# A cross-attention and expert kernel on one core: eight constant matmuls for ten, VectorE for all low parts of the query weights, and a new order on every engine

## The chip, the core and the metric

The kernel runs on one core of a Trainium2 chip. The metric is the device time of one execution in microseconds (us), taken over repeated runs; the core has five engines that matter here: TensorE (PE in the profile, with its weight loads as PEld), VectorE (DVE), ScalarE (ACT), GpSimd (POOL) and SyncE (SP), which only issues the DMAs. The engines run their own instruction streams in order and meet through semaphores.

## What is computed

A block of cross-attention with a residual, and then a small mixture of experts with a residual, for x of 4 x 512 x 512 and a context of 4 x 64 x 512, in float32. Cut to what matters:

```python
h  = layernorm(x)                                  # over 512 features
q  = h @ Wq.T + bq ; k = ctx @ Wk.T + bk ; v = ctx @ Wv.T + bv     # 16 heads of 32
s  = clip(q k / sqrt(32), -50, 50), -10000 where masked, clip again
c  = softmax(s) v
d  = rs * (c @ Wo.T + bo)
x1 = x + (d - mean(d)) / sqrt(var(d) + eps) * gamma + beta
n  = layernorm(x1)
g  = softmax(n @ router.T), kept for the 2 largest of 8 experts
x2 = x1 + sum over experts of g_e * silu(n @ down_e.T) @ up_e
```

## The kernel before

The rows of x are taken in four batches of four tiles of 128 rows; `f(b, t)` below is step f for batch b and tile (or chunk, or half) t. All data stay in SBUF. A float32 product that has to be exact enough is made of three passes of the rounded type fp32r: operands are split into a high part (ACT casts, `hs_hi`, `wq_high`, `att_hi`) and a low part (a subtraction, `hs_lo`, `wq_low`, `wo_low`, `att_lo`), and `passes` issues hi x hi, hi x lo and lo x hi for each of four chunks: 12 matmuls of 128 x 512 for `query` and for `project`.

The order of the start on PE: WARM constant matmuls of 128 x 128 on the tile `average` (float32, so two passes each), `keys(c)` and `values(c)` for the four chunks of context weights, the transposes of the normalised tiles of batch 0 (`hs_transpose`, at L496), then `query(0, 0..3)`, then the transposes of batch 1, `scores(0, 0)`, `expert_means` and `scores(0, 1)`, and `query(1, 0)`. `query(b, 0)` waits for all four low parts of the batch (`hst_lo`, written at L1119 by VectorE for batches 0 and 1), and for all four `wq_lo` chunks.

On VectorE the start is: the cleaning of the context (`clean_marks`, `clean_limited`, `clean_finite`), the layernorm statistics (`tile_stats`, L1262 and L1264), `hs_lo(0, t)`, the mask (`mask_limits`), two of the four `wq_low` (L1284), the statistics of batch 1, the centring of the output weights in place (`centre_wo(c)`, whose last step is L1274), the blocks of values (`value_blocks`, L1163), `hs_lo(1, t)` and the clipping of the exponentiated scores (`clip`, L1178). GpSimd forms the other two `wq_low` (L1584), adds beta to the residual in place (`add_beta`, L1530) after its DMA, raises variances to the power -1/2 (`ln_power`), and forms `up_lo`, `wo_lo` and `attt_lo` (L1589, L1579, L1534).

Each engine's order is written out by hand, call by call. The eight PSUM banks are handed from use to use by the table `BANKS`: a row is a bank, a name a use (K keys, Q query, S scores, W projection, U and E experts' up products, h, n, a transposes, V values, m means, s sums, v weighed values, f down products), and a use may begin when the engine that reads out the use before it is done (`take`, and `seed` for W and E). Where the names are on one row, one waits for the other:

```python
        def take(use):
            before = banks.before(use)
            if before:
                pe.wait_ge(freeing[before[0]], banks.count(before))
            return bank(use)
```

Lines that the steps below touch: L635 constant matmuls, L529 keys, L539 values, L496 transposes, L478 all matmuls that `passes` issues, L555 scores, L569 sums, L1119, L1163, L1178, L1262, L1274, L1284 on VectorE, L1530, L1584 on GpSimd.

## Time and profile before

| | |
|---|---|
| median of 3 runs | 182.28 us (182.18 to 182.46) |
| the profiled execution, its own time | 181.53 us |
| its span in the profile | 179.7 us |
| busy: PE, DVE, ACT, POOL | 171.3, 133.0, 118.5, 106.7 us |
| share of the chain that ended last: PE, DVE | 51%, 26% |
| granted TensorE clock | 1.00 over nearly all of the span |

The span goes from the first to the last record of the profiled execution; 1.83 us of that execution's time lie outside it. Times in the rows are counted from the start of the span. A row of the timeline has start, length, engine, line, operation, what is written <- what is read, and in brackets how long the engine sat idle before and what it waited for. Two neighbouring instructions of one engine may overlap by some 0.07 us, so four of a kind take a little less than four times one.

### The profile page before, as it was taken

The numbers are of one execution on the slowest core, as the hardware profiler recorded it, in microseconds if no ns is written. First come the engines' busy times: TensorE is split into PE (matmuls) and PEld (weight loads), VectorE is DVE, ScalarE is ACT, GpSimd is POOL, SyncE is SP. The second block draws the span as 40 slices with busy tenths as digits, with TensorE's granted clock in tenths as the row PEclk, the third lists the DMA queues.
The fourth block names the chain that finished last, engine by engine and source line by source line (L and its number), as shares of the span: only waits on it lengthen the run. The fifth ranks groups of instructions, "written<-read, shape, count | busy, mean of one in ns | idle before, by whom it ended". The sixth has DMA issues, their size and how long they took to land.

```text
span 179.7 us, 3565 instructions
## 1 busy us (share of the span) xinstructions
PE 171.3 (95%) x1212; PEld 126.2 (70%) x1212; DVE 133.0 (74%) x300; ACT 118.5 (66%) x239; POOL 106.7 (59%) x159
## 2 busy tenths in 40 slices
PE   7999899978999999999999999999999999999992
PEld 7766578646845477688788687657876688889861
DVE  3695999997999389769148784075999985877891
ACT  3038818865736768469998575379935767688852
POOL 6042899974765617999987983066143692385200
PEclk9999999999999999999999999999999999999999
DMA  4999993000249974355990248621143598001068
GB/s 161 329 395 368 383 357 121 0 0 4 53 151 305 314 160 135 117 181 205 311 227 14 119 133 252 175 60 62 26 109 127 181 330 254 2 2 58 2 226 303
DMA packets 18050, 30.14 MB, mean 168 GB/s; under 512 B 3056, under 2 KB 8176, under 8 KB 17776
## 3 DMA queue, kind: packets, MB, share of 16 engines
q1 hardware_dynamic: 18032, 29.92, 51.5%
q8 instruction: 10, 0.16, 0.4%
q14 instruction: 8, 0.07, 0.1%
HBM read 19.95 MB, written 9.96 MB: 166 GB/s over the span
## 4 chain that ended last, share of the span: by engine, by line
PE 51%; DVE 26%; DMA 8%; SPq 7%; issue 3%; ACT 2%; POOL 1%; DVEq 0%; ACTq 0%
PE ps L478 43%; DMA mask_sb<-mask_t 4%; DVE ln_st L1262 2%; PE ps L555 2%; PE ps L569 2%; DVE stage L1178 2%; DVE hst_lo L1119 2%; DMA x_scratch<-x_turned 2%; DVE rz L1183 2%; DVE v_sb L1163 2%; DVE wq_lo L1284 2%; PE ps L583 2%; PE ps L496 2%; DMA x_turned<-x_scratch 2%; DVE xs L1274 1%
## 5 line engine op out<-in xcount | busy, mean ns | idle before, releaser
L478 PE MATMUL ps<-hst_hi,wq_hi 128*128 128x512 f32 x64 | 25.9, 405 | 1.7 <-DVE hst_lo L1119 1.7
L1534 POOL TENSOR_TENSOR attt_lo<-wk,attt_hi 128x512 fp32r<-128x512 f32 x16 | 21.1, 1346 | 9.6 <-ACT attt_hi L813 9.6
L478 PE MATMUL ps<-wo_hi,attt_hi 128*128 128x512 f32 x64 | 26.0, 406 | 0.3 <-POOL attt_lo L1534 0.3
L478 PE MATMUL ps<-wo_hi,attt_lo 128*128 128x512 f32 x64 | 25.3, 395 | 0.0
L478 PE MATMUL ps<-hst_lo,wq_hi 128*128 128x512 f32 x64 | 25.3, 395 | 0.0
L478 PE MATMUL ps<-hst_hi,wq_lo 128*128 128x512 f32 x64 | 25.3, 395 | 0.0
L478 PE MATMUL ps<-wo_lo,attt_hi 128*128 128x512 f32 x64 | 25.3, 395 | 0.0
L1530 POOL TENSOR_TENSOR xs<-xs,beta_bc 128x512 f32<-128x512 f32 x16 | 20.7, 1324 | 1.7 <-ACT hs L776 0.9
L1178 DVE TENSOR_SCALAR stage<-stage,exp_max 128x1024 f32<-128x1024 f32 x16 | 13.9, 881 | 8.8 <-ACT stage L795 8.8
L776 ACT ACTIVATE hs<-xs,ln_bias,ln_rstd 128x512 f32<-128x512 f32 x16 | 12.1, 808 | 11.8 <-POOL ln_bias L1522 11.8
L795 ACT ACTIVATE stage<-ps 128x1024 f32<-128x1024 f32 x16 | 16.1, 1021 | 4.4 <-PE ps L555 4.4
L478 PEld LDWEIGHTS ps<-hst_hi,wq_hi 128*128 128x128 f32 x64 | 12.0, 188 | 8.3 <-issue 3.6
L782 ACT ACTIVATE q_sb<-ps,bq_sb 128x512 f32<-128x512 f32 x16 | 10.7, 682 | 9.9 <-PE ps L478 9.8
L478 PEld LDWEIGHTS ps<-dr_raw,x1t 128*128 128x128 f32 x128 | 15.5, 190 | 1.7 <-issue 1.1
L1549 POOL TENSOR_SCALAR d_ve<-d_sq,rs_sq 128x1 f32<-128x1 f32 x16 | 4.6, 289 | 20.3 <-ACT cen L876 19.9
L478 PE MATMUL ps<-dr_raw,x1t 128*128 128x136 f32 x128 | 16.3, 282 | 0.1
L1188 DVE TENSOR_TENSOR wk<-ps,wk 128x512 f32<-128x512 f32 x16 | 10.4, 677 | 7.3 <-PE ps L583 6.3
L478 PEld LDWEIGHTS ps<-wo_hi,attt_hi 128*128 128x128 f32 x64 | 12.0, 188 | 4.2 <-issue 1.7
L1205 DVE SCALAR_TENSOR_TENSOR xs<-cen,d_rstd,xs 128x512 f32<-128x512 f32 x16 | 11.9, 748 | 3.7 <-POOL d_rstd L1552 3.7
L813 ACT CAST attt_hi<-wk 128x512 fp32r<-128x512 f32 x16 | 9.7, 620 | 7.0 <-DVE wk L1188 4.8
L876 ACT ACTIVATE cen<-ps 128x512 f32<-128x512 f32 x16 | 9.5, 594 | 6.9 <-PE ps L478 6.6
L478 PEld LDWEIGHTS ps<-hst_hi,wq_lo 128*128 128x128 f32 x64 | 12.0, 188 | 2.8
(114 smaller groups left out, 395.6 us busy)
## 6 DMA issues: line engine op xcount, KB each, us to landing
wk<-rz_scratch SPq DMA_DIRECT2D x32, 128.0 KB, 2.8
out<-xs SPq DMA_DIRECT2D x16, 256.0 KB, 2.6
xs<-x SPq DMA_DIRECT2D x3, 1024.0 KB, 8.4
x_scratch<-x_turned SPq DMA_DIRECT2D x6, 512.0 KB, 2.6
x_turned<-x_scratch SPq DMA_DIRECT2D x24, 128.0 KB, 2.8
hs_scratch<-hs_turned SPq DMA_DIRECT2D x2, 1024.0 KB, 4.6
hs<-hs_scratch SPq DMA_DIRECT2D x8, 256.0 KB, 5.6
wk<-wk_t SPq DMA_DIRECT2D x4, 256.0 KB, 6.5
```

The lines of the kernel that those rows point to most:

```text
L478: last = pe.matmul(dst, w, m, start=start and i == 0, stop=stop and i == n - 1, skip_group_check=unseen)
L776: act.activation(hs[:, t, :], xs[:, bass.ds(tile, 1), :], ACT.Identity, bias=ln_bias[:, bass.ds(tile, 1)], scale=ln_rstd[:, bass.ds(tile, ...
L782: act.activation(q_sb[:, m, :], bank(f"Q{b}{m}"), ACT.Identity, bias=bq_sb[:, m:m + 1]).then_inc(q_ok, 1)
L795: act.activation(probs[:, 2 * c:2 * c + 2, :], bank(f"S{b}{2 * c}", 2).rearrange("p (c n) -> p c n", c=2), ACT.Exp, scale=SCALE).then_inc( ...
L813: act.copy(attt_hi[:, :, c, :], att[:, c, :].rearrange("p (t n) -> p t n", t=NT)).then_inc(attt_hi_ok, 1)
L876: act.activation(cen[:, t, :], bank(f"W{b}{t}"), ACT.Square, accum_out=d_sq[:, NT * b + t:NT * b + t + 1]).then_inc(d_sq_ok, 1)
L1178: dve.tensor_scalar(probs[:, ps, :], probs[:, ps, :], EXP_LO, exp_max[:, b:b + 1], ALU.max, ALU.min).then_inc(probs_ok, 1)
L1188: dve.tensor_tensor(att[:, c, :], bank(f"v{b}{c}"), att[:, c, :], ALU.mult).then_inc(weighed_out, 1)
L1205: dve.scalar_tensor_tensor(x_tile, cen[:, t, :], d_rstd[:, NT * b + t:NT * b + t + 1], x_tile, ALU.mult, ALU.add, accum_out=n_sum[:, NT * ...
L1530: pool.tensor_tensor(xt, xt, beta_bc[:, :], ALU.add).then_inc(xb_ok, 1)
L1534: pool.tensor_tensor(attt_lo[:, :, c, :], att[:, c, :].rearrange("p (t n) -> p t n", t=NT), attt_hi[:, :, c, :].bitcast(F32), ALU.subtract ...
L1549: pool.tensor_scalar(d_ve[:, NT * b + t:NT * b + t + 1], d_sq[:, NT * b + t:NT * b + t + 1], rs_sq[:, :], EPS, ALU.mult, ALU.add).then_inc ...
```

## The change

1. WARM is 8, was 10.
2. The last two `wq_low` chunks move from GpSimd to VectorE, which now forms all four; `wq_low(0)` stands ahead of `mask_limits`, the other three behind it.
3. New orders. On PE `keys(2)` moves ahead of `hs_transpose(0, 0)`, `scores(0, 1)` ahead of `expert_means`, and some steps of the later batches change places by one to three positions; on ACT, VectorE and GpSimd likewise. SP swaps one fetch with one send of reciprocals.
4. New rows in `BANKS`. The uses of late batches sit on other banks; `U12 U13 U20 U22` now follow each other on one bank.

The arithmetic is that of before: same operations, same shapes, apart from the two constant matmuls whose result nobody reads.

```diff
-WARM = 10
+WARM = 8
...
-    "K3 S00 S05 Q12 S13 S16 W03 S20 W11 S26 Q33 S33 S36 W23 U10 W32 U13 U22",
+    "K2 Q03 S04 Q11 S12 S15 W02 Q23 W10 S25 Q32 S32 S36 W23 U10 W32 U12 U13 U20 U22",
...
             keys(1)
+            keys(2)
             hs_transpose(0, 0)
-            keys(2)
...
+            scores(0, 1)
             expert_means()
-            scores(0, 1)
...
             hs_norm(0, 1)
+            hs_norm(0, 2)
             hs_hi(0, 0)
-            hs_norm(0, 2)
...
             clean_marks(3)
-            hs_lo(0, 0)
             clean_limited(3)
             clean_finite(3)
+            hs_lo(0, 0)
             hs_lo(0, 1)
+            wq_low(0)
             mask_limits()
-            wq_low(0)
             wq_low(1)
+            wq_low(2)
+            wq_low(3)
...
             ln_power(2, 4)
-            wq_low(2)
-            wq_low(3)
             add_beta(0, 0)
```

VectorE between the context cleaning and the statistics of batch 1; `hst_lo` are the low parts of the normalised tiles of batch 0, `dr_raw` and `compare` hold the context's marks and its clean copy, `attend` and `exp_max` are the mask. The first fence is before, the second the changed kernel.

```order
L1119 TENSOR_TENSOR hst_lo<-ps,hst_hi 128x512
L1301 COPY_PREDICATED compare<-dr_raw,hidden 128x256
L1305 COPY_PREDICATED compare<-dr_raw,stage 128x256
L1119 TENSOR_TENSOR hst_lo<-ps,hst_hi 128x512
L1309 TENSOR_SCALAR attend<-mask_sb 128x4
L1311 TENSOR_SCALAR exp_max<-attend 128x4
L1284 TENSOR_TENSOR wq_lo<-stage,wq_hi 128x512 x2
L1119 TENSOR_TENSOR hst_lo<-ps,hst_hi 128x512 x2
```

```order
L1301 COPY_PREDICATED compare<-dr_raw,hidden 128x256
L1305 COPY_PREDICATED compare<-dr_raw,stage 128x256
L1119 TENSOR_TENSOR hst_lo<-ps,hst_hi 128x512 x2
L1284 TENSOR_TENSOR wq_lo<-stage,wq_hi 128x512
L1309 TENSOR_SCALAR attend<-mask_sb 128x4
L1311 TENSOR_SCALAR exp_max<-attend 128x4
L1284 TENSOR_TENSOR wq_lo<-stage,wq_hi 128x512 x3
L1119 TENSOR_TENSOR hst_lo<-ps,hst_hi 128x512 x2
```

VectorE has two more subtractions here, and `hst_lo` of tile 0 stands behind the cleaning of the last context chunk instead of inside it.

VectorE from the statistics of batch 2 to the clipping of batch 0's scores (`stage`); the `hst_lo` are now those of batch 1.

```order
 L1262 BN_STATS ln_st<-xs 128x6
 L1264 BN_AGGR ln_mv<-ln_st 128x2
-L1119 TENSOR_TENSOR hst_lo<-ps,hst_hi 128x512
-L1178 TENSOR_SCALAR stage<-stage,exp_max 128x1024
-L1119 TENSOR_TENSOR hst_lo<-ps,hst_hi 128x512 x2
-L1178 TENSOR_SCALAR stage<-stage,exp_max 128x1024
-L1262 BN_STATS ln_st<-xs 128x6
-L1264 BN_AGGR ln_mv<-ln_st 128x2
-L1178 TENSOR_SCALAR stage<-stage,exp_max 128x1024 x2
+L1178 TENSOR_SCALAR stage<-stage,exp_max 128x1024
+L1119 TENSOR_TENSOR hst_lo<-ps,hst_hi 128x512 x3
+L1262 BN_STATS ln_st<-xs 128x6
+L1264 BN_AGGR ln_mv<-ln_st 128x2
+L1178 TENSOR_SCALAR stage<-stage,exp_max 128x1024 x3
```

The first clip moves ahead of `hs_lo(1, 1)`, and the second behind the statistics of the last tile of batch 2.

## Rows read from the trace of the kernel before

**Rows 1.** Page: busy time by engine, and the chain's shares by engine.
```profile
PE 171.3 (95%) x1212; PEld 126.2 (70%) x1212; DVE 133.0 (74%) x300; ACT 118.5 (66%) x239; POOL 106.7 (59%) x159
PE 51%; DVE 26%; DMA 8%; SPq 7%; issue 3%; ACT 2%; POOL 1%; DVEq 0%; ACTq 0%
```
**Rows 2.** Stretches: start:end, length, busy us (instructions) by engine, granted clock, DMA.
```profile
30.00:40.00 10.00, 8.91 (x74) 6.18 (x72) 9.58 (x19) 8.48 (x14) 9.29 (x8) 1.00 0.01 2
62.00:172.00 110.00, 109.83 (x785) 83.94 (x785) 78.99 (x192) 80.83 (x181) 66.34 (x100) 1.00 0.45 137
```
**Rows 3.** PE's longest wait in all, over the whole span: us, times, longest.
```profile
PE ps L478 <- DVE hst_lo L1119: 2.4, 3, 1.0
```
**Rows 4.** Timeline of PE, the first 13 us.
```profile
1.05 4.63 PE L635 MATMUL ps<-average 128*128 128x128 f32 x20 [1.05 <-POOL average L1592]
5.47 1.93 PE L529 MATMUL ps<-compare,wk 128*128 128x256 f32 x8
11.00 1.99 PE L529 MATMUL ps<-compare,wk 128*128 128x256 f32 x8 [0.17 <-DMA wk<-wk_t]
```
**Rows 5.** Timeline of DVE, POOL, ACT and PE around the query weights.
```profile
17.63 0.17 DVE L1309 TENSOR_SCALAR attend<-mask_sb 128x4 f32<-128x4 int32 x1 [0.68 <-DMA mask_sb<-mask_t]
17.91 3.46 DVE L1284 TENSOR_TENSOR wq_lo<-stage,wq_hi 128x512 fp32r<-128x512 f32 x2
17.86 2.96 POOL L1584 TENSOR_TENSOR wq_lo<-stage,wq_hi 128x512 fp32r<-128x512 f32 x2 [3.17 <-ACT wq_hi L894]
19.51 1.07 ACT L759 CAST hst_hi<-ps 128x512 fp32r<-128x512 f32 x2 [0.51 <-PE ps L496]
21.29 1.27 DVE L1119 TENSOR_TENSOR hst_lo<-ps,hst_hi 128x512 fp32r<-128x512 f32 x2
19.74 1.89 PE L529 MATMUL ps<-compare,wk 128*128 128x256 f32 x8
22.66 0.47 PE L478 MATMUL ps<-hst_hi,wq_hi 128*128 128x512 f32 x1 [1.03 <-DVE hst_lo L1119]
```
**Rows 6.** Groups of one line: ns min/median/max, first and last start.
```profile
L1294 DVE TENSOR_TENSOR dr_raw<-stage x4: 414/418/420, 3.4 to 13.2; 128x256 uint8<-128x256 f32 x4
```
**Rows 7.** Timeline of DVE and POOL, 21 to 32 us.
```profile
21.62 5.02 POOL L1530 TENSOR_TENSOR xs<-xs,beta_bc 128x512 f32<-128x512 f32 x4 [0.80 <-DMA beta_bc<-beta]
26.66 0.49 DVE L1274 TENSOR_SCALAR xs<-xs,w_mv 128x512 f32<-128x512 f32 x1
29.12 1.29 POOL L1589 TENSOR_TENSOR up_lo<-hidden,up_hi 128x512 fp32r<-128x512 f32 x1
29.49 1.22 DVE L1274 TENSOR_SCALAR xs<-xs,w_mv 128x512 f32<-128x512 f32 x1
```
**Rows 8.** Timeline of POOL, DVE and PE, 36 to 42 us.
```profile
36.79 2.50 POOL L1579 TENSOR_TENSOR wo_lo<-xs,wo_hi 128x512 fp32r<-128x512 f32 x2
36.14 0.69 DVE L1119 TENSOR_TENSOR hst_lo<-ps,hst_hi 128x512 fp32r<-128x512 f32 x1
38.14 1.71 DVE L1178 TENSOR_SCALAR stage<-stage,exp_max 128x1024 f32<-128x1024 f32 x1
39.77 1.27 DVE L1119 TENSOR_TENSOR hst_lo<-ps,hst_hi 128x512 fp32r<-128x512 f32 x2
38.28 1.19 PE L478 MATMUL ps<-dr_raw,average 128*128 128x136 f32 x8 [0.67 <-DVE hst_lo L1119]
41.19 0.47 PE L478 MATMUL ps<-hst_hi,wq_hi 128*128 128x512 f32 x1 [0.67 <-DVE hst_lo L1119]
```
**Rows 9.** Timeline of POOL, DVE and PE, 46 to 62 us.
```profile
46.19 5.07 POOL L1530 TENSOR_TENSOR xs<-xs,beta_bc 128x512 f32<-128x512 f32 x4 [0.93 <-ACT hs L776]
49.92 1.63 DVE L1274 TENSOR_SCALAR xs<-xs,w_mv 128x512 f32<-128x512 f32 x1
61.77 0.47 PE L478 MATMUL ps<-wo_hi,attt_hi 128*128 128x512 f32 x1 [0.26 <-POOL attt_lo L1534]
```
**Rows 10.** Timeline of PE at the end.
```profile
172.90 0.44 PE L496 MATMUL ps<-ident,hidden 128*128 128x128 f32 x2 [0.31 <-DVE hidden L1245]
```

More of the change, by code:

```diff
@@ L707, in _ @@
             project(2, 1)
+            weigh(3, 0)
             sums(3, 1)
             project(2, 2)
-            weigh(3, 0)
+            project(2, 3)
             hid_transpose(0, 1)
-            project(2, 3)
+            weigh(3, 1)
             up(0, 1)
             hid_transpose(1, 0)
-            weigh(3, 1)
             up(0, 2)
@@ L735, in _ @@
             x1_transpose(3, 2)
+            up(1, 2)
             down(3, 0)
             down(3, 1)
+            up(1, 3)
+            x1_transpose(3, 3)
+            hid_transpose(2, 1)
             down(3, 2)
-            x1_transpose(3, 3)
-            up(1, 3)
-            hid_transpose(2, 1)
             down(3, 3)
@@ L931, in _ @@
             exp_scores(0, 0)
+            exp_scores(0, 1)
             hs_hi(1, 1)
[L933 removed]
             hs_hi(1, 2)
@@ L986, in _ @@
             exp_scores(2, 0)
+            exp_scores(2, 1)
             seed(1, 1)
             seed(1, 2)
-            exp_scores(2, 1)
             seed(1, 3)
             x1_out(0, 2)
+            down_scaled(0, 0)
             projected_squares(1, 0)
-            down_scaled(0, 0)
+            x1_out(0, 3)
             down_scaled(0, 1)
-            x1_out(0, 3)
+            hidden_tanh(0, 0)
             exp_logits(0, 0)
-            hidden_tanh(0, 0)
             projected_squares(1, 1)
@@ L1012, in _ @@
             x1_out(1, 0)
+            x1_out(1, 1)
+            hid_hi(0, 0)
+            query_out(3, 1)
             x1_squares(1, 3)
-            query_out(3, 1)
-            x1_out(1, 1)
             query_out(3, 2)
             query_out(3, 3)
+            exp_scores(3, 0)
             att_hi(2, 0)
             att_hi(2, 1)
-            exp_scores(3, 0)
+            exp_scores(3, 1)
+            down_scaled(0, 2)
             att_hi(2, 2)
             att_hi(2, 3)
-            down_scaled(0, 2)
+            down_scaled(0, 3)
             x1_out(1, 2)
-            exp_scores(3, 1)
             x1_out(1, 3)
+            hidden_tanh(0, 1)
             seed(2, 0)
-            down_scaled(0, 3)
-            hidden_tanh(0, 1)
             exp_scores(3, 2)
@@ L1067, in _ @@
             projected_squares(3, 0)
+            x1_squares(2, 3)
             x1_out(2, 2)
@@ L1070, in _ @@
             x1_out(2, 3)
+            experts_seed(2, 3)
             projected_squares(3, 1)
-            x1_squares(2, 3)
-            experts_seed(2, 3)
+            x1_squares(3, 0)
+            projected_squares(3, 2)
+            x1_squares(3, 1)
+            experts_seed(3, 1)
+            x1_squares(3, 2)
             hid_hi(1, 1)
-            projected_squares(3, 2)
-            x1_squares(3, 0)
-            x1_squares(3, 1)
             hid_hi(2, 0)
+            down_scaled(2, 2)
             projected_squares(3, 3)
-            down_scaled(2, 2)
-            x1_squares(3, 2)
             down_scaled(2, 3)
@@ L1085, in _ @@
             x1_out(3, 1)
+            x1_out(3, 2)
             exp_logits(2, 1)
-            x1_out(3, 2)
+            experts_seed(3, 2)
+            down_scaled(3, 0)
             x1_squares(3, 3)
-            down_scaled(3, 0)
             down_scaled(3, 1)
@@ L1365, in _ @@
             tile_stats(2, 2)
+            clip(0, 0)
             hs_lo(1, 1)
-            clip(0, 0)
             hs_lo(1, 2)
             hs_lo(1, 3)
+            tile_stats(2, 3)
             clip(0, 1)
-            tile_stats(2, 3)
             clip(0, 2)
@@ L1404, in _ @@
             product(1, 0)
+            product(1, 1)
             residual(0, 1)
@@ L1423, in _ @@
             residual(1, 0)
-            gating(0, 0)
+            x1_turn(1, 0)
             scaled(1, 1)
-            x1_turn(1, 0)
-            scaled(1, 2)
             residual(1, 1)
             x1_turn(1, 1)
+            scaled(1, 2)
+            gating(0, 0)
             scaled(1, 3)
-            reciprocals(2, 0)
             residual(1, 2)
             clip(2, 2)
+            reciprocals(2, 0)
+            clip(2, 3)
             x1_turn(1, 2)
-            clip(2, 3)
+            residual(1, 3)
             hid_lo(0, 0)
-            residual(1, 3)
             x1_turn(1, 3)
@@ L1441, in _ @@
             product(2, 1)
+            clip(3, 0)
             product(2, 2)
             product(2, 3)
-            clip(3, 0)
+            clip(3, 1)
             finish(0, 0)
-            clip(3, 1)
             largest(0, 1)
@@ L1465, in _ @@
             residual(2, 2)
+            hid_lo(0, 1)
             x1_turn(2, 2)
             scaled(2, 3)
+            product(3, 2)
             hid_lo(1, 0)
-            product(3, 2)
             finish(0, 1)
+            product(3, 3)
             finish(0, 2)
-            product(3, 3)
             residual(2, 3)
@@ L1627, in _ @@
             add_beta(1, 2)
+            wo_low(1)
             add_beta(1, 3)
-            wo_low(1)
             wo_low(2)
```

51 lines of the change are left out of this document (22 added, 29 removed), and 14 rows, old and new, of the table BANKS.

## The prediction, written before the changed kernel was run

> **What bounds the kernel now.** I read the page's busy times and chain first, then the busy time by stretch, then TensorE's waits, then the timelines of the places where it waits. TensorE is busy for 171.3 of 179.7 us and carries 51% of the chain that ended last; VectorE carries another 26% [rows 1]. The stretches say where each of the two rules. From 62 to 172 us TensorE is busy for 109.83 of 110 us, so in there an order can only lose time, never gain it [rows 2]. What can be gained is ahead of that: from 30 to 40 us TensorE is busy for 8.91 us and VectorE for 9.58 [rows 2], and nearly all that TensorE waits for is `hst_lo`, VectorE's low parts of the normalised rows: 2.4 us in three waits [rows 3], at 22.66, 38.28 and 41.19 us [rows 5, 8]. One more short wait for `attt_lo` ends at 61.77 [rows 9], and one for the gating at 172.90 [rows 10]. So the sum is made at two points: when `query(0, 0)` starts (22.66) and when `query(1, 0)` starts (41.19), and after that at the start of the projections (61.77).
>
> **Two constant matmuls fewer.** Twenty passes take 4.63 us, 0.23 each [rows 4], so four fewer take 0.9 us off TensorE's first work. The keys' first matmuls can move forward by that at most, but the second chunk of key weights lands only at 11.00, where TensorE already waits 0.17 us for it [rows 4]; the gain ends there. Worth nothing on the path: the cover is that DMA, and if the DMA came earlier the gain would be up to 0.9. The passes still run until about 4.8, and the keys follow with hardly a hole, so TensorE is as busy as before when it reaches its steady pace.
>
> **All low parts of the query weights on VectorE.** Before, VectorE takes 3.46 us for two chunks, 1.73 each, while GpSimd takes 2.96 us for its two over the same time [rows 5]. With GpSimd out of there, what does one cost? The nearest row is the comparison of a context chunk with itself, also two float32 inputs from SBUF, of 256 elements: 418 ns [rows 6]; the subtraction of 512 elements from PSUM takes 0.69 alone and 1.27 for a pair, 0.61 in a series [rows 8, 5]. Lower end 0.61, upper end 1.73 (that of before, if the length were the instruction's own); I take 0.61 to 0.7, since the 418 ns are twice 0.21, and 512 elements at that rate are under 0.84.
> The row says that the two engines' subtractions hold each other up. The Trainium skill (SBUF — State Buffer, section "Who interferes with whom") states the rule: a VectorE instruction with two SBUF inputs contends with a GpSimd instruction that reads SBUF, and one waits until the other is through. By that rule a chunk is short once GpSimd is silent; without it the upper end would stand.
> Then the step: one chunk fits into the 0.68 us that VectorE idled ahead of the mask, three stand behind the mask, which ends at 18.0 [rows 5]. 18.0 + 3 x 0.61 to 0.7 = 19.8 to 20.1. The last two high parts are done at 20.58 [rows 5], the first of them at about 20.1, and each `hs_lo` takes 0.61: 21.35 to 21.5. Placing `keys(2)` ahead of the transposes delays ScalarE's casts of the weights by some 0.3 us and not its last two. TensorE itself is through with the last keys at 19.74 + 1.89 = 21.63 [rows 5]. So TensorE becomes what ends last, and `query(0, 0)` starts at 21.6 to 21.8: 0.9 to 1.0 us earlier. VectorE is ahead of its old place by 22.56 - 21.4 = 1.1 us.
>
> **GpSimd is not earlier for it.** It loses 2.96 us of work, but its next step, `add_beta(0, 0)`, waited 0.80 us for beta, which lands at 21.6 [rows 7]. So its four additions of 1.25 us still run from 21.62 to 26.64 with no hole.
>
> **What VectorE's lead meets.** `centre_wo(0)` ends in a scalar subtraction that took 0.49 us at 26.66, just after these additions, and 1.22 at 29.49, when `up_lo` ran on GpSimd until 30.41 [rows 7]: this operation, too, waits for GpSimd. 1.1 us earlier it comes at 25.5, and the fourth addition runs from 25.37 to 26.64. So it waits until 26.64 and VectorE's lead is gone: it reaches the values' blocks at 30.6 as before. TensorE, ahead by 1.0, then waits that much longer for the slot that `hs_lo(1, 0)` frees at 36.8 [rows 8]. The order of the statistics and values changes nothing in that sum.
>
> **Clip ahead of `hs_lo(1, 1)`.** Before, the first clip comes at 38.2, meets `wo_low` and takes 1.71 us, to 39.85, of which only the 0.56 after GpSimd's end at 39.29 can be work; the last two `hs_lo` follow from 39.77 to 41.04 and `query(1, 0)` at 41.19 [rows 8]. Now the clip comes at 37.55. GpSimd is full of additions and subtractions of 1.25 us until 39.29, and the next border between two of them is at 38.05 [rows 8]. In the pair of query weights the engines took turns at such borders, so I let the clip in there: 38.05 to 38.65, then three `hs_lo` of 0.61, 40.5. `expert_means` (1.19 us) needs the first of these, at 39.3, and is through at 40.5 as well; `scores(0, 1)` now fills its wait of 0.67 [rows 8]. `query(1, 0)` starts at 40.55: 0.64 earlier. Bounds: 1.76 + 1.03 = 2.8 us earlier if VectorE never held TensorE (1.76 is the 1.09 us of TensorE's idle time from 30 to 40 us [rows 2] and the 0.67 at 41.19; 1.03 the wait at 22.66 [rows 5]), 0.55 later if the clip gets in only at 39.29.
>
> **To the projections.** VectorE's next steps start with TensorE's sums and move with it. `centre_wo(3)` at 49.92 took 1.63 us because `add_beta(2, ...)` held it until 51.26 [rows 9]; its statistics are now ready earlier, so these additions start some 1.2 us earlier and end at 50.1, and the subtraction is through at 50.6 instead of 51.55. VectorE is ahead by 0.8 to 0.9 for the products, and `attt_lo` with it, so the wait of 0.26 at 61.77 goes [rows 9]: the projections start 0.64 + 0.2 = 0.85 us earlier.
>
> **The rest.** Up to 172 us TensorE has no hole, and I find none that the new order opens: the transposes of `hidg` and the up products change places with work that was ready, and `down` and `x1_transpose` keep their order of arrival. In the tail `up(1, 3)`, `up(2, 0)` and `up(2, 2)` now follow on one bank, so `up(2, 2)` waits some 0.25 us for VectorE's addition of tile (2, 0); it lies in front of the wait of 0.31 us for the gating [rows 10] and is hidden by it. If the gating came earlier it would cost its 0.25. Moved or swapped fetches on SP's queue: nothing, while their waits are for data and not for the queue.
>
> Sum: 181.53 - 0.85 = 180.7 for an execution like the profiled one. That one lies 0.75 us below the median of 182.28, so the median becomes 182.28 - 0.85 = 181.4.
>
> **Rivals.**
> (a) The subtraction of `centre_wo(0)` slips in ahead of the fourth `add_beta`. For it: 25.37 and 25.5 are 0.1 us apart, and the landing of beta moves by more. Then VectorE is at the values' blocks at about 29.1 instead of 30.6, `query(1, 0)` at 39.7, and with the projections the gain is 1.5 + 0.3 = 1.8: 180.5. 20%.
> (b) Slower: the clip stands ahead of three `hs_lo`, and GpSimd lets it in only when its row of work ends at 39.29. Then `hs_lo(1, 3)` is done at 41.7, `query(1, 0)` starts 0.55 later and nothing returns it: 182.8. It decides from a stay of 0.6 us beyond 38.05. Against it: the two engines took turns at 17.9 to 21.4. 12%.
> (c) Slower: a chunk of `wq_lo` takes its 1.73 us by itself. Then from 16.95, where VectorE began to idle ahead of the mask, four chunks (6.9), the mask (0.35) and two `hs_lo` (1.2) end at 25.4 instead of 22.56 [rows 5]; VectorE stays behind by 2.9 until 41, less 0.64 for the clip's place: 184.5. It decides above 1.2 us a chunk, where the four eat up the 0.64. Against it stand the 418 ns [rows 6]. 8%.
> (d) No difference: the 0.85 is there at 61.77 and a changed order in the late batches opens holes of some tenths under a full TensorE, or the lead before 61.77 shrinks to below 0.36. Nothing in the rows shows such a hole, but 100 us of new order with 70 to 80% busy VectorE and ScalarE give room for one [rows 2]. 182.2. 17%.
>
> **Chances.** My own case holds 43% (180.8 to 182.0 by its terms). A measurement of this kernel can tell 0.2%, 0.36 us. Faster by more than that: my case nearly whole, and (a): 0.63. Within: (d) and a rest: 0.17. Slower: (b), (c): 0.20. The range reaches from a little below (a) to (b): 180.2 to 182.9.
>
> **What would show it.** Right: L1284 four times at under 0.8 us, TensorE's wait ahead of `query(0, 0)` at nearly nothing, start near 21.7; the first L1274 long (1.2 us or more) and the first clip of 1.1 us; `query(1, 0)` near 40.55; the projections without their wait. Wrong: L1284 near 1.7 each, a first L1274 of 0.49 at 25.5 (then (a)), a clip over 2 us (then (b)), or a stretch from 61 to 171 in which TensorE is busy for less than all of it but 0.2 us (then (d)).

## The result: slower by 1.7%, with the profile after

The changed kernel takes 185.11 us (median of 6 runs, 184.6 to 186.11) against 182.37 us of the kernel before on the same chips; the ratio is 1.017, with a 95% interval from 1.013 to 1.021. The forecast was 181.4 us, with a range up to 182.9. Its profiled execution took 185.09 us, with a span of 183.4 us (before 179.7), at a granted clock of 1.00 in each of the stretches below. Medians here are over all executions of a kernel, while each ratio and its interval leave out those in the chip's slower state and take the kernel before in the same rounds, so the two can differ by some tenths of a per cent.

The page of the changed kernel, busy time by engine:

```profile
PE 171.9 (94%) x1208; PEld 125.8 (69%) x1208; DVE 134.6 (73%) x302; ACT 117.4 (64%) x239; POOL 104.1 (57%) x157
```

TensorE is as busy as before to 0.6 us [rows 1]; the span is 3.7 us longer. So the time is waiting, not work. The stretches of the changed kernel tell where (length, busy us of PE, PEld, DVE, ACT, POOL, clock, DMA):

```profile
62.00:100.00 38.00, 37.71 (x219) 28.78 (x218) 26.26 (x48) 29.95 (x64) 29.94 (x40) 1.00 0.56 162
100.00:120.00 20.00, 18.47 (x174) 11.91 (x181) 12.05 (x23) 9.01 (x18) 8.56 (x15) 1.00 0.51 161
120.00:160.00 40.00, 39.52 (x303) 30.29 (x288) 32.00 (x82) 29.72 (x70) 21.66 (x34) 1.00 0.39 125
160.00:172.00 12.00, 11.12 (x83) 10.18 (x82) 8.67 (x31) 9.54 (x26) 5.87 (x13) 1.00 0.09 35
```

From 62 to 172 us TensorE is now busy for 106.8 us of 110; before it was 109.83 [rows 2]. The lead of the start is there, 0.64 us at the projections for the 0.85 forecast, and it is lost in this stretch, with more. TensorE's waits in the changed kernel, by what it waited for (us in total, times, longest; the wait of 1.0 us for `average` ahead of the first matmul, the same in both, and those of under 0.5 us are left out):

```profile
PE ps L496 <- DVE hidden L1245: 1.4, 1, 1.4
PE ps L478 <- DVE hidt_lo L1119: 0.9, 1, 0.9
PE ps L478 <- DVE hst_lo L1119: 0.6, 1, 0.6
PE ps L496 <- DVE hst_lo L1119: 0.6, 1, 0.6
PE ps L555 <- ACT q_sb L782: 0.6, 1, 0.6
PE ps L478 <- POOL attt_lo L1536: 0.5, 2, 0.3
```

The matmuls of L478 wait 0.6 us for `hst_lo` where they waited 2.4 [rows 3]; the transposes of L496 wait 0.6 us for it, before 0.4. Three of these waits did not exist before: one for the gated hidden values, at 104 us, one for `hidt_lo`, at 164 us, and one for `q_sb` ahead of the scores at 34 us.

The start, in the changed kernel, to be read beside [rows 5, 7, 8]:

```profile
18.76 1.89 DVE L1284 TENSOR_TENSOR wq_lo<-stage,wq_hi 128x512 fp32r<-128x512 f32 x3
21.95 0.47 PE L478 MATMUL ps<-hst_hi,wq_hi 128*128 128x512 f32 x1
22.11 5.05 POOL L1532 TENSOR_TENSOR xs<-xs,beta_bc 128x512 f32<-128x512 f32 x4 [6.78 <-DMA beta_bc<-beta]
25.94 1.50 DVE L1274 TENSOR_SCALAR xs<-xs,w_mv 128x512 f32<-128x512 f32 x1
37.70 1.18 DVE L1178 TENSOR_SCALAR stage<-stage,exp_max 128x1024 f32<-128x1024 f32 x1
40.81 0.47 PE L478 MATMUL ps<-hst_hi,wq_hi 128*128 128x512 f32 x1
```

A low part of the query weights takes 0.63 us (three in 1.89), `query(0, 0)` starts without a wait for `hst_lo`, the first long step of `centre_wo` is stretched to 1.50 by GpSimd's additions, and the clip takes 1.18 us.

The best way to read the rest is TensorE's lead: the start of the same matmul, less its start before. The lead is 0.71 us at `query(0, 0)`, 0.38 at `query(1, 0)`, and 0.65 at 87 us. Then it goes in four steps. TensorE's timeline in the changed kernel at these steps:

```profile
89.48 0.51 PE L478 MATMUL ps<-wo_hi,attt_hi 128*128 128x512 f32 x1 [0.29 <-POOL attt_lo L1536]
104.33 0.44 PE L496 MATMUL ps<-ident,hidden 128*128 128x128 f32 x2 [1.37 <-DVE hidden L1245]
122.71 3.05 PE L478 MATMUL ps<-dr_raw,x1t 128*128 128x136 f32 x24 [0.23 <-DVE wk L1188]
164.16 1.19 PE L478 MATMUL ps<-dr_raw,x1t 128*128 128x136 f32 x8 [0.88 <-DVE hidt_lo L1119]
```

**First**, at 89 us: 0.65 ahead becomes 0.14. ScalarE now squares two tiles between the casts of batch 2, so GpSimd's `hst_lo(2, ...)` pause for 0.51 us after the first, and everything on GpSimd down to `attt_lo(1, 3)` keeps that. **Second**, at 104 us: 0.14 ahead becomes 1.69 behind. `gating(0, 0)` stands five steps later on VectorE. The timeline of VectorE and GpSimd in the changed kernel, where `hidden` is what the gating works on:

```profile
97.02 5.68 POOL L1542 TENSOR_TENSOR hst_lo<-hs,hst_hi 128x512 fp32r<-128x512 f32 x4
97.18 1.68 DVE L1205 SCALAR_TENSOR_TENSOR xs<-cen,d_rstd,xs 128x512 f32<-128x512 f32 x1 [0.17 <-POOL d_rstd L1554]
100.12 1.45 DVE L1220 SCALAR_TENSOR_TENSOR hidden<-hidden 128x256 f32<-128x256 f32 x1
101.49 1.36 DVE L1224 TENSOR_TENSOR compare<-compare,least 128x128 f32<-128x128 f32 x1
103.85 0.42 DVE L1245 TENSOR_TENSOR hidden<-hidden,gate 128x256 f32<-128x256 f32 x1 [0.26 <-DVE gate L1238]
```

In the kernel before the same two steps were over just ahead of GpSimd's four subtractions:

```profile
95.67 0.41 DVE L1220 SCALAR_TENSOR_TENSOR hidden<-hidden 128x256 f32<-128x256 f32 x1
96.00 0.28 DVE L1224 TENSOR_TENSOR compare<-compare,least 128x128 f32<-128x128 f32 x1
97.20 5.63 POOL L1540 TENSOR_TENSOR hst_lo<-hs,hst_hi 128x512 fp32r<-128x512 f32 x4
```

So 0.69 us of work became 2.81. **Third**, at 122 us: 1.7 behind becomes 2.1, with a short wait of 0.23 us for a product. **Fourth**, at 164 us: 1.9 behind becomes 2.8. ScalarE's cast `hid_hi(1, 1)` and VectorE's `hid_lo(1, 1)` stand behind two squares that wait for VectorE; in the changed kernel:

```profile
160.29 0.72 ACT L884 ACTIVATE cen<-xs,n_sum 128x512 f32<-128x512 f32 x1 [0.45 <-DVE xs L1205]
162.58 0.72 ACT L884 ACTIVATE cen<-xs,n_sum 128x512 f32<-128x512 f32 x1 [1.00 <-DVE xs L1205]
163.30 0.62 ACT L759 CAST hidt_hi<-ps 128x256 fp32r<-128x256 f32 x2
163.69 0.76 DVE L1119 TENSOR_TENSOR hidt_lo<-ps,hidt_hi 128x256 fp32r<-128x256 f32 x2 [1.14 <-ACT hidt_hi L759]
```

The last addition to x starts at 179.16 us, 2.83 later than before (176.33), and the rest of the 3.7 is in the stores: 4.2 us from there to the end of the span instead of 3.4. No run looked into why the stores take longer.

### The profile page after: what moved, and what is told of

Read it like the earlier page. It is cut to its first block, busy times and chain, and to the rows that moved or that the text cites. A ratio compares the mean times of both kernels' runs of the same rounds, so it can differ in the third digit from the quotient of the medians.

```text
span 183.4 us, 3557 instructions
## 1 busy us (share of the span) xinstructions
PE 171.9 (94%) x1208; PEld 125.8 (69%) x1208; DVE 134.6 (73%) x302; ACT 117.4 (64%) x239; POOL 104.1 (57%) x157
## 4 chain that ended last, share of the span: by engine, by line
PE 25%; DVE 23%; DMA 20%; POOL 13%; SPq 7%; issue 6%; ACT 4%; DVEq 0%; ACTq 0%; POOLq 0%
PE ps L478 20%; SPq L365 4%; DMA hs<-hs_scratch 4%; DVE ln_st L1262 4%; DMA x_scratch<-x_turned 3%; DMA rz_scratch<-rz 3%; POOL xs L1532 3%; DMA hs_scratch<-hs_turned 3%; POOL attt_lo L1536 3%; DMA stage<-ctx_t 3%; DMA x_turned<-x_scratch 2%; POOL hst_lo L1542 2%; DVE hst_lo L1119 2%; DMA wk<-rz_scratch 2%; POOL d_rstd L1554 2%
## 5 line engine op out<-in xcount | busy, mean ns | idle before, releaser
L478 PE MATMUL ps<-wo_hi,attt_hi 128*128 128x512 f32 x64 | 25.8, 404 | 0.5 <-POOL attt_lo L1536 0.5
L478 PE MATMUL ps<-hst_hi,wq_hi 128*128 128x512 f32 x64 | 25.9, 405 | 0.4 <-DVE cen L1197 0.2
L478 PE MATMUL ps<-wo_hi,attt_lo 128*128 128x512 f32 x64 | 25.3, 395 | 0.0
L478 PE MATMUL ps<-hst_hi,wq_lo 128*128 128x512 f32 x64 | 25.3, 395 | 0.0
L478 PE MATMUL ps<-wo_lo,attt_hi 128*128 128x512 f32 x64 | 25.2, 394 | 0.0
L478 PE MATMUL ps<-hst_lo,wq_hi 128*128 128x512 f32 x64 | 25.2, 394 | 0.0
L1178 DVE TENSOR_SCALAR stage<-stage,exp_max 128x1024 f32<-128x1024 f32 x16 | 13.1, 836 | 9.3 <-ACT stage L795 9.3
L478 PE MATMUL ps<-dr_raw,x1t 128*128 128x136 f32 x128 | 16.7, 282 | 1.4 <-DVE hidt_lo L1119 0.9
L478 PEld LDWEIGHTS ps<-dr_raw,x1t 128*128 128x128 f32 x128 | 15.7, 190 | 3.0 <-issue 1.2
L478 PEld LDWEIGHTS ps<-hst_hi,wq_hi 128*128 128x128 f32 x64 | 12.0, 188 | 5.7 <-issue 2.3
L478 PEld LDWEIGHTS ps<-wo_hi,attt_hi 128*128 128x128 f32 x64 | 12.0, 188 | 4.8 <-issue 1.7
L1205 DVE SCALAR_TENSOR_TENSOR xs<-cen,d_rstd,xs 128x512 f32<-128x512 f32 x16 | 13.0, 810 | 3.0 <-POOL d_rstd L1554 3.0
L1197 DVE TENSOR_TENSOR cen<-ps,gamma_bc 128x512 f32<-128x512 f32 x16 | 10.8, 676 | 4.8 <-ACT cen L876 4.8
L478 PEld LDWEIGHTS ps<-wo_hi,attt_lo 128*128 128x128 f32 x64 | 12.0, 188 | 2.9
L478 PEld LDWEIGHTS ps<-hst_hi,wq_lo 128*128 128x128 f32 x64 | 12.0, 188 | 2.8
```

The costliest lines, as they stand in the source:

```text
L478: last = pe.matmul(dst, w, m, start=start and i == 0, stop=stop and i == n - 1, skip_group_check=unseen)
L1178: dve.tensor_scalar(probs[:, ps, :], probs[:, ps, :], EXP_LO, exp_max[:, b:b + 1], ALU.max, ALU.min).then_inc(probs_ok, 1)
L1197: dve.tensor_tensor(cen[:, t, :], bank(f"W{b}{t}"), gamma_rs[:, :], ALU.mult).then_inc(w_free, 1)
L1205: dve.scalar_tensor_tensor(x_tile, cen[:, t, :], d_rstd[:, NT * b + t:NT * b + t + 1], x_tile, ALU.mult, ALU.add, accum_out=n_sum[:, NT * ...
```

## The experiments

Each comparison is with the kernel before, run in between on the same chip. This table, made from all the traces, is what most verdicts rest on. It gives the start of the same matmul less its start in the kernel before, in us; negative is ahead. A single execution's head start is uncertain: e5 and e12, whose start is that of the kernel before, begin `query(0, 0)` 0.59 and 1.44 us earlier than it, and e12 is still 0.87 ahead at the projections. So the steps from column to column count more than the level. e2, e6 and e8 are left out; the executions profiled of e2 and e8 were the slowest of each (188.73 and 183.55 us). The matmul at 103.24 us is the first of `query(3, 0)`; the expectation of e9 calls it `query(2, 0)`, but that one starts at 75 us.

| kernel | query(0,0) 22.66 | query(1,0) 41.19 | project(0,0) 61.77 | project(1,0) 89.62 | query(3,0) 103.24 | project(2,0) 125.67 | up 143.05 | last up 175.43 |
|---|---|---|---|---|---|---|---|---|
| changed | -0.71 | -0.38 | -0.64 | -0.14 | +1.69 | +2.07 | +1.94 | +2.84 |
| e1 head alone | -0.67 | -1.06 | -1.35 | -1.33 | -0.68 | -0.64 | -0.63 | -0.75 |
| e3 gating back | -1.01 | -0.90 | -1.16 | -1.05 | -1.08 | -0.29 | -0.42 | +0.70 |
| e4 query weights alone | -0.73 | 0.00 | 0.00 | -0.03 | +0.67 | +0.64 | +0.65 | +0.64 |
| e5 gating alone | -0.59 | +0.01 | 0.00 | -0.03 | +1.55 | +1.83 | +1.85 | +1.71 |
| e7 three back | -0.67 | -1.03 | -1.31 | -1.33 | -1.36 | -0.46 | -0.59 | +0.97 |
| e9 square | -0.36 | -0.98 | -1.26 | -1.24 | -1.25 | -0.68 | -0.68 | -0.78 |
| e10 square, spread | -1.13 | -1.54 | -1.82 | -1.79 | -1.80 | -1.81 | -1.80 | -2.13 |
| e11 banks back too | -1.14 | -0.64 | -0.93 | -0.95 | -0.99 | +0.07 | -0.07 | -0.01 |
| e12 tail alone | -1.44 | -0.85 | -0.87 | -0.90 | -0.91 | -0.93 | -0.92 | +0.30 |

**e1, the head alone.** Only the part up to 60 us: two constant matmuls fewer, all `wq_low` on VectorE, and the orders there.

> The kernel before with the first part of the change only: eight constant matmuls, all four low parts of the query weights on VectorE, and the new order of every engine up to the scores of batch 0; the bank table and all later orders as before. Theory (the start of the change is worth what was forecast, and the later orders lose it): query(0, 0) starts near 21.9, query(1, 0) near 40.8, the projections near 61.1, the rest keeps that lead, 0.6 us faster than before. Rival (the lead is lost anyway behind 62 us, since GpSimd's chain sets the start of batch 1's projections): within 0.2 us of before. Rival (the start itself costs what the changed kernel lost): 1 to 3 us slower.

```diff
-WARM = 10
+WARM = 8
...
+            wq_low(0)
             mask_limits()
-            wq_low(0)
             wq_low(1)
+            wq_low(2)
+            wq_low(3)
...
+            clip(0, 0)
             hs_lo(1, 1)
-            clip(0, 0)
```

Measured: 182.02 us, ratio 0.998 (0.994 to 1.002), a gain that this many runs can't tell from none. In the trace TensorE is 1.35 us ahead at the projections, keeps it to 89 us, loses half of it at 102 us and is 0.75 ahead at the last up product. The head therefore costs nothing, and the second rival falls; all of the loss is in the moves behind 60 us.

**e2, all but the head.** The rest of the change without the part that e1 holds.

> The changed kernel with its first part taken back: ten constant matmuls, two low parts of the query weights on GpSimd, and the order of before up to the scores of batch 0; bank table and later orders are those of the change. Theory (the later orders lose the time): 3.0 to 3.7 us slower than before, TensorE again waiting 1.4 us for the gated hidden values at about 105 us and 0.9 us for hidt_lo at about 165. Rival (the losses come from the lead of the start colliding with GpSimd): within 1 us of before.

```diff
             projected_squares(0, 0)
             hs_hi(2, 0)
+            projected_squares(0, 1)
+            x1_squares(0, 0)
             hs_hi(2, 1)
...
-            gating(0, 0)
...
+            gating(0, 0)
...
-            hid_lo(1, 1)
...
+            hid_lo(1, 1)
```

Measured: 186.13 us, ratio 1.019 (1.011 to 1.026), which is 3.4 us and within the theory's range. Without the head the loss is all there, at least as large as in the changed kernel, and TensorE waits behind 60 us for the same three things, `attt_lo`, `hidden` and `hidt_lo`.

**e3, the gating put back** in the changed kernel.

> The changed kernel with one step moved back: on VectorE gating(0, 0) stands again right behind residual(1, 0), ahead of x1_turn(1, 0) and scaled(1, 1). Theory (behind those it meets GpSimd's hst_lo of batch 3, and TensorE waits for it): its two long operations fall from 1.45 and 1.36 us to about 0.4 and 0.3, TensorE's wait of 1.37 us ahead of the transpose of hidden goes, and the kernel is 1.3 to 1.6 us faster than the changed one. Rival (TensorE then waits for the scores' clips, sums or banks instead): under 0.4 us faster.

```diff
+            gating(0, 0)
+            scaled(1, 1)
             x1_turn(1, 0)
-            scaled(1, 1)
+            scaled(1, 2)
             residual(1, 1)
             x1_turn(1, 1)
-            scaled(1, 2)
-            gating(0, 0)
```

Measured: 183.7 us, ratio 1.008 (1.005 to 1.012): 1.4 us of the loss is gone. In its trace L1220 and L1224 are 0.41 and 0.28 us long again and the wait for `hidden` is not there: 1.08 ahead at 103 us where the changed kernel is 1.69 behind. But the lead does not last. TensorE in that kernel:

```profile
120.35 3.05 PE L478 MATMUL ps<-dr_raw,x1t 128*128 128x136 f32 x24 [0.66 <-DVE wk L1188]
162.03 1.19 PE L478 MATMUL ps<-dr_raw,x1t 128*128 128x136 f32 x8 [1.21 <-DVE hidt_lo L1119]
```

**e4, the query weights alone**: the kernel before with VectorE forming all four low parts, in the new order around the mask.

> The kernel before with the low parts of the query weights alone: all four on VectorE, hs_lo(0, 0) behind the context's cleaning, nothing else changed. Theory: the subtractions of 512 elements take 0.68 us each, query(0, 0) starts 0.7 to 1.0 us earlier, and VectorE's lead is eaten by the first centre_wo waiting for add_beta, so that query(1, 0) starts within 0.2 us of 41.19 and the time is within 0.3 us of before. Rival (TensorE keeps its lead): 0.6 to 1.0 us faster.

```diff
-            hs_lo(0, 0)
...
+            hs_lo(0, 0)
             hs_lo(0, 1)
+            wq_low(0)
             mask_limits()
-            wq_low(0)
             wq_low(1)
+            wq_low(2)
+            wq_low(3)
```

Measured: 182.11 us, ratio 1.000 (0.997 to 1.003). `query(0, 0)` is 0.73 earlier, no more than e5 and e12 show without this edit, and `query(1, 0)` not at all. That fits the theory. VectorE in that kernel:

```profile
25.93 1.27 DVE L1274 TENSOR_SCALAR xs<-xs,w_mv 128x512 f32<-128x512 f32 x1
100.15 1.55 DVE L1205 SCALAR_TENSOR_TENSOR xs<-cen,d_rstd,xs 128x512 f32<-128x512 f32 x1
```

The first row is the wait for GpSimd's additions that eats the lead. The second is at a place that the edit does not touch: in the kernel before this step took 0.77 us at 99.67, in the same row of GpSimd's `hst_lo`, but it came 0.2 us ahead of the border between two of them; here it came 0.3 us behind a border, and TensorE lost 0.65 us at 103. So the same subtractions of GpSimd can cost time even in an order that was left alone, on a difference of tenths in arrival.

**e5, the gating alone**, in the kernel before.

> The kernel before with only the gating of (0,0) moved: on VectorE behind x1_turn(1,0), scaled(1,1), residual(1,1), x1_turn(1,1) and scaled(1,2), and hid_transpose(0,0) two places later on TensorE, as the change has both. Theory (collision): its first two steps (L1220 and L1224, 0.41 and 0.28 us before) now run beside GpSimd's four hst_lo of batch 3 and take 1.3 to 1.5 us each, so hidden is ready at about 104.5 us, TensorE stands 1.2 to 1.7 us ahead of the hidden transposes, and nothing behind gives it back: 183.6 to 184.2 us against 182.25. Rival (the two steps were long only because other moves of the change had made the neighbourhood late): they stay near 0.41 and 0.28 us, the hole is under 0.4 us, 182.2 to 182.6 us.

```diff
-            hid_transpose(0, 0)
...
+            hid_transpose(0, 0)
...
-            gating(0, 0)
-            scaled(1, 1)
             x1_turn(1, 0)
-            scaled(1, 2)
+            scaled(1, 1)
             residual(1, 1)
             x1_turn(1, 1)
+            scaled(1, 2)
+            gating(0, 0)
```

Measured: 183.73 us, ratio 1.006 (1.003 to 1.009), 1.3 us slower. VectorE and TensorE in that kernel:

```profile
100.21 1.44 DVE L1220 SCALAR_TENSOR_TENSOR hidden<-hidden 128x256 f32<-128x256 f32 x1
101.57 1.36 DVE L1224 TENSOR_TENSOR compare<-compare,least 128x128 f32<-128x128 f32 x1
104.19 0.44 PE L496 MATMUL ps<-ident,hidden 128*128 128x128 f32 x2 [1.15 <-DVE hidden L1245]
```

The collision theory holds: the same stretched pair and the same hole, with nothing else of the change in place. TensorE is 1.55 behind at 103 us and 1.71 at the end. The rival, that these steps were long only because the neighbourhood was late, falls.

**e6, the orders behind 150 us put back** in the changed kernel.

> The changed kernel with the orders of all engines behind 150 us put back. Theory (losses in series, each with its own place): the wait for hidt_lo at 164 us (0.9 us in the changed kernel) goes and those at 104 us (1.4) and 123 us (0.2) stay: 183.9 to 184.4 us against 185.11 of the changed kernel. Rival (the wait at 164 us is only the late gating handed on): it comes back at another place behind 150 us and the time is within 0.3 us of 185.1.

```diff
-            x1_squares(3, 2)
...
+            x1_squares(3, 2)
...
+            hid_lo(1, 1)
...
-            hid_lo(1, 1)
```

Measured: 186.24 us, ratio 1.015 (1.008 to 1.022), not the 184 that the theory gave; its five runs spread from 184.1 to 187.8, and the ratio rests on three of them (184.1, 185.0 and 186.2), so the times say little and the trace more. The rival's time, 185.1, lies among them. The wait for `hidt_lo` is gone, and two others stand in its place. TensorE in that kernel:

```profile
169.23 1.19 PE L478 MATMUL ps<-dr_raw,x1t 128*128 128x136 f32 x8 [0.46 <-ACT hidden L847]
173.53 0.47 PE L478 MATMUL ps<-up_hi,hidt_hi 128*128 128x512 f32 x1 [0.68 <-DVE xs L1254]
```

This looked like the rival, a delay handed on. It was not: the table of banks was still the new one, made for the new order. e7 and e11 test that.

**e7, three groups put back**: the gating, ScalarE's casts of batch 2, and the orders behind 150 us.

> The changed kernel with three groups put back at once: the gating of (0,0), ScalarE's high parts of hs(2,1..3), and the orders behind 150 us. Theory (these three are the whole loss): the gain of the head is left, 181.9 to 182.5 us, and no wait of TensorE over 0.3 us behind 60 us besides the one for cen at 102 us. Rival (the other moves between 60 and 150 us, such as spread_in(2,1) and product(2,2), cost by themselves): a wait of 0.4 to 0.7 us for wk at 120 us stays, and the time is 182.6 to 183.3 us.

```diff
+            hs_hi(2, 1)
+            hs_hi(2, 2)
             projected_squares(0, 1)
+            hs_hi(2, 3)
             x1_squares(0, 0)
-            hs_hi(2, 1)
-            hs_hi(2, 2)
-            hs_hi(2, 3)
```

Measured: 183.73 us, ratio 1.005 (1.002 to 1.009). With the casts back GpSimd forms the four `hst_lo` of batch 2 in one piece, and `project(1, 0)` starts with no wait:

```profile
66.98 5.06 POOL L1542 TENSOR_TENSOR hst_lo<-hs,hst_hi 128x512 fp32r<-128x512 f32 x4 [1.19 <-ACT hst_hi L806]
120.18 3.05 PE L478 MATMUL ps<-dr_raw,x1t 128*128 128x136 f32 x24 [0.78 <-DVE wk L1188]
166.10 1.19 PE L478 MATMUL ps<-dr_raw,x1t 128*128 128x136 f32 x8 [0.46 <-ACT hidden L847]
170.40 0.47 PE L478 MATMUL ps<-up_hi,hidt_hi 128*128 128x512 f32 x1 [0.69 <-DVE xs L1254]
```

TensorE is 1.36 us ahead at 103 us, the best so far, and then two places take it: the product at 120 us, and the tail with the same pair of waits as in e6 although it is 3.1 us earlier there than in e6. So those don't come from lateness. The theory, that the three groups are the whole loss, falls; of the rival the wait for `wk` came (0.78 us), and the time is above its range because of the tail.

**e8 and e9, one square moved.** In e1 TensorE waited 0.60 us at 102.56 for a centring, which waited for ScalarE's square of the projection, which stood behind the square of a late `xs`. The edit to e1's kernel, measured twice, the second time for a trace of a usual execution:

> The changed head alone, and on ScalarE projected_squares(1,3) ahead of x1_squares(1,1). In the head alone TensorE waits 0.60 us at 102.56 us for a centring, which waits for that square, which stands behind the square of an xs that VectorE brings late (1.63 us for 0.77, beside GpSimd's hst_lo). Theory: this order hands the head's lead of 1.3 us through to the end: the wait is under 0.1 us, the last up product starts 0.5 us earlier (174.6 us), 181.4 to 181.7 us against 182.0 of the head alone. Rival: VectorE's own queue (x1_turn(1,1) stands ahead of the centring) brings it late anyway, or the next wait takes it: within 0.15 us of the head alone.

> The changed head with projected_squares(1,3) ahead of x1_squares(1,1), once more, for a profile that shows where its gain of the first measurement (181.08 us) comes from. Theory: no wait for cen at 102 us, query(2,0) starts at 101.9 to 102.1 us (102.56 in the head alone), and some of that lead is lost again at 118 to 123 us to a wait for wk, whose transfer does not depend on this. Rival: the wait for cen stays or moves to another bank, and the measured gain was the state of the chip.

```diff
-            x1_squares(1, 1)
             projected_squares(1, 3)
+            x1_squares(1, 1)
```

Measured: 181.08 us, ratio 0.995 (0.991 to 0.998), and again 180.83 us, ratio 0.990 (0.987 to 0.994). It beats the kernel before both times; against the head alone it is less sure, since the interval of e1, 0.994 to 1.002, overlaps that of e8. In e9's trace the wait for the centring is gone and TensorE is 1.25 ahead at 103 us, where e1 had 0.68; between 118 and 125 us it comes down to 0.68, the product that it then waits for being this one:

```profile
118.96 1.29 DVE L1188 TENSOR_TENSOR wk<-ps,wk 128x512 f32<-128x512 f32 x2 [1.85 <-DMA wk<-rz_scratch]
```

So of e8's theory the wait went, and the 0.5 us at the last up product did not come: as its rival said, the next wait took it. The two profiled executions of e1 and e9 start their last up product at the same time (174.68 and 174.65 us), while the medians are 0.9 to 1.2 us apart. So the traces show how e9 is ahead at 103 us, not why its usual run is that much faster; that part stays open.

**e10, the reciprocals' transfer ahead of a fetch**, on top of e9.

> The same, and on SyncE spread_in(2,1) ahead of x1_fetch(1,1). Theory: with the gating put back, TensorE's lead over the kernel before fell from 1.12 us at 117 us to 0.29 us at 125 us, behind a product that waited for wk<-rz_scratch, which is issued behind x1_fetch(1,1). Issued first it lands about 1.7 us earlier, so a lead of 1.3 us stays whole: last up product at 174.0 to 174.3 us, 180.5 to 180.9 us. Rival: the scratch transfer is bound by its own send or x1t(1,1) comes late in its turn: the same as without it, within 0.2 us.

```diff
             spread_out(2, 1)
-            x1_fetch(1, 1)
             spread_in(2, 1)
+            x1_fetch(1, 1)
```

Measured: 180.47 us (6 runs), ratio 0.990 (0.984 to 0.996). The kernel description above says that all data stay in SBUF, which is not so: the reciprocals, the turned x and the turned normalised rows go out to scratch in DRAM (`rz_scratch`, `x_scratch`, `hs_scratch`) and come back, and the first of these is what the product waits for. SyncE's queue in e9, and then in e10:

```profile
112.25 1.75 SPq L386 DMA_DIRECT2D x_turned<-x_scratch  x4
114.10 1.76 SPq L365 DMA_DIRECT2D wk<-rz_scratch  x4
```

```profile
111.73 1.71 SPq L365 DMA_DIRECT2D wk<-rz_scratch  x4
113.48 1.86 SPq L386 DMA_DIRECT2D x_turned<-x_scratch  x4
```

The transfer is issued 2.4 us earlier, no product waits for it, and the lead of 1.80 us passes 125 us whole: the theory that this transfer sets the earliest time of the product holds. Of the 2.13 us at the last up product only 1.3 reach the span (178.4 against 179.7), for the stores take longer: 4.2 us from the last addition to the end, before 3.4. Against e9 the 0.36 us between the medians can't be told from nothing.

**e11, the table of banks put back too**, on top of e7.

> The changed kernel with the three groups put back (gating, ScalarE's high parts, the orders behind 150 us) and also the table of banks. Theory: the 0.46 us for hidden at 166 us and the 0.69 us for xs at 170 us that came up when only the orders behind 150 us were put back are waits for banks that the new table gives to other groups; with the old table both go, the last up product starts at 174.8 to 175.1 us instead of 176.4 us, 182.1 to 182.6 us against 183.73. Rival: they come from ScalarE and VectorE being late by themselves, and stay: 183.4 to 184.0 us.

```diff
-    "V1 h12 s00 v00 v03 s10 s11 v12 f01 s21 v22 f03 s30 v30 v32 f12 f21 f22 n31 f31 f32 a30",
+    "V1 h12 s00 v00 v03 s10 s11 v12 f01 s21 v22 f03 s30 s31 a01 a10 f12 f21 f22 n31 f31 a21 a31",
```

Measured: 181.72 us, ratio 0.995 (0.991 to 0.998). From 143 us to the end the lead stays where it is (-0.07, -0.01), where e7 lost 1.56; the waits for `hidden` and `xs` are gone. The old order behind 150 us needs the old table.

e11 and e12, the next run, also say where the third loss comes from. At 103 us they are almost equally far ahead (0.99 and 0.91), and at 125 us e11, with the new order between 60 and 150 us, has lost 1.06, e12 with the old one nothing. In both VectorE takes `hid_lo(0, 0)` ahead of the last turning of batch 1's x, `x1_turn(1, 3)`. In e11 it waits there for ScalarE's cast `hid_hi(0, 0)`, which the new order puts behind six more steps; the first row is e11, the second e12:

```profile
108.40 0.42 DVE L1119 TENSOR_TENSOR hidt_lo<-ps,hidt_hi 128x256 fp32r<-128x256 f32 x1 [1.04 <-ACT hidt_hi L759]
106.17 0.42 DVE L1119 TENSOR_TENSOR hidt_lo<-ps,hidt_hi 128x256 fp32r<-128x256 f32 x1
```

The send of the turned x, its fetch and then the reciprocals' transfer follow later on SyncE's queue: the last is issued at 114.80 us in e11 and at 113.78 in e12. No run moved this cast alone, so this cause is read from two traces and not shown by an edit.

**e12, the tail alone**: the kernel before with the orders behind 150 us and the table of banks of the change.

> The kernel before with nothing but the change's orders behind 150 us and its table of banks. Theory: they cost by themselves what the trace of the changed kernel shows at 164 us, a wait for hidt_lo of 0.8 to 1.2 us with no gating or head moved: 183.1 to 183.6 us against 182.4. Rival: order and table fit each other, and the wait at 164 us needs the lateness from 104 us: no wait over 0.3 us there and 182.2 to 182.6 us.

```diff
-    "V0 h11 m0 v01 v10 v13 a00 v21 f02 f11 v31 v33 f20 a20 n30 f30 n33 f33",
+    "V0 h11 m0 v01 v10 v13 s20 v20 v23 f10 v31 v33 f20 a20 n30 f30 a21",
...
+            x1_squares(3, 1)
+            experts_seed(3, 1)
+            x1_squares(3, 2)
...
-            hid_lo(1, 1)
...
+            hid_lo(1, 1)
```

Measured: 183.67 us, ratio 1.003 (0.999 to 1.007), by the runs alone not resolved. The trace is clear: 0.92 ahead at 143 us, 0.30 behind at the end, through this one wait:

```profile
161.61 1.19 PE L478 MATMUL ps<-dr_raw,x1t 128*128 128x136 f32 x8 [1.38 <-DVE hidt_lo L1119]
```

The new tail makes its own hole, with no gating moved and a TensorE that is early. Its rival falls. The old tail with its own table has no such hole (e1, e11), nor has the old tail with the new table (e6, e7), so it comes from the order. The new order with the old table was not run.

## Why the prediction was wrong, step by step

**Right, with sizes.** The two constant matmuls are worth nothing by themselves. `wq_lo` costs 0.63 us alone, inside the 0.61 to 0.7; rival (c) is dead. `query(0, 0)` starts at 21.95 (21.6 to 21.8 forecast, 22.66 before), a little late since the keys ahead of it were. How much of this is the edit one trace can't tell: the two `wq_lo` on VectorE that took 3.46 us in the kernel before [rows 5] took 2.36 and 2.38 in e5 and e12, in the same order, and `query(0, 0)` started 0.59 and 1.44 us earlier there too. VectorE's lead is eaten at `centre_wo(0)`: 1.50 us at 25.94, until GpSimd's four additions are over at 27.16 (26.64 forecast; they began 0.5 us later). e4 shows the same by itself, and rival (a) didn't come about. The clip took 1.18 us and was through at 38.88, so rival (b) didn't either. `query(1, 0)` started at 40.81, against 40.55 forecast, and at 40.13 in e1 with the same head. The head's 0.85 us at the projections measured 0.64 in the changed kernel, and 0.93 to 1.82 in the others with this head; but e12, without it, was 0.87 ahead there and e5 not at all, so the size is not shown. By the runs the whole head (e1) is worth anything from 1.1 us to a loss of 0.3. The wait for `attt_lo` at 61 us, though, did not go (0.25 us in every kernel): GpSimd's chain moved earlier by as much as TensorE. The wait of `up(2, 2)` for its bank, forecast as 0.25 us and hidden by the wait for the gating behind it, is there: TensorE falls back by 0.3 us at 171 and has it again at 173. The Trainium skill (SBUF — State Buffer, section "Who interferes with whom") was the source for `wq_lo` being short once GpSimd is silent, and the 0.63 us agree.

**Wrong: the step named "The rest".** It says that TensorE "has no hole and I find none that the new order opens". There were four. Two are shown by edits of their own: the gating moved into GpSimd's subtractions, 1.8 us at 104 us in the changed kernel and 1.55 alone (e5, and gone in e3); the late casts and low parts of the tail, 0.9 and alone 1.2 (e12). The other two were never moved alone: ScalarE's casts of batch 2, 0.5 (gone in e7, where they are put back with two other groups; with GpSimd's same pause of 0.5 us TensorE lost 0.1 in e3 and 0.4 in e6), and the product, 0.4 (0.8 to 1.1 in e3, e7 and e11, where TensorE comes to it earlier). Less the 0.65 of the head that is the 2.84 us at the last up product. 1.83 + 0.51 + 0.38 - 0.13 + 0.90 = 3.49, and 3.49 - 0.65 = 2.84. The other 0.87 of the span is the stores, a term that the prediction did not have and whose cause stays open.

The failure was in reading, not in a missing row. The stretch at 109.83 of 110 us [rows 2] was taken to mean that only short holes could open there. With no hole in TensorE its row says nothing about how near the other engines are to late; that has to be read from their own rows, move by move. For the gating the rows were there, in the trace of the kernel before. It ended at 97.48 us, 3.4 us ahead of its reader, and its new place was beside a GpSimd that subtracts from 97.20 to 102.83. As an estimate from these rows: at their old lengths the five steps ahead of it would have been over at about 99.7 (the last of them started at 99.06, behind ScalarE's square, and takes 0.69), the gating's 1.8 us would have ended at 101.5, and TensorE, whose order puts the transposes later too, comes for them at about 103.0 (104.33 less the wait of 1.37): harmless. It was the 3.0 us of waiting for GpSimd, 2.1 in the pair L1220 and L1224 and 0.9 in the L1205 ahead of them, that made the hole of 1.37.

The prediction had the rule for this, and used it ahead of 62 us only: for `wq_lo`, for both `centre_wo` steps and for the clip. The Trainium skill (SBUF — State Buffer, section "Who interferes with whom") states it for every VectorE instruction with two SBUF inputs beside a GpSimd instruction that reads SBUF. By it each step of the pair waits until the subtraction under way is through. Both come just behind the start of one, so an estimate for each is nearly a whole subtraction and its own work, about 5.68 / 4 = 1.4 us, 2.8 for the two; the trace agrees, with 2.81.

**Rival (d)** named the right kind, holes under a full TensorE from a new order in the late batches, but sized them to cancel 0.85 us where they were 3.5, and gave it 17%. The bound should have come from the moves, each with its distance to its reader and what stands in its new slot.

## What to carry to other kernels

In a stretch where the bounding engine has no hole, list for every moved step its end, its reader's start and the length of what it is moved behind; a move longer than that distance is a loss, whatever the order was made for. When a VectorE step with two SBUF operands is moved, look up what GpSimd does in its new slot; by the estimate above that alone turned a harmless move into a hole here, where beside a row of GpSimd subtractions a step of 0.28 us took 1.36. An order and its table of banks are one edit: the old order behind 150 us lost 1.56 us with the new table and nothing with its own (e7 against e11), so undoing half of such an edit gives a false verdict. And look at more than one trace of an unchanged stretch before a difference of under 1 us in it is called the edit's.
